# Busy matmuls and moved moments in the lead-in between two attentions

## The chip, the core and the metric

One NeuronCore of a Trainium2 chip runs the whole kernel. The metric is the device time of one execution in microseconds; the figure shown is the median of three runs. Five engines work side by side and meet at semaphores: TensorE (PE) multiplies, VectorE (DVE) and ScalarE (ACT) do elementwise work and reductions, GpSimd (POOL) helps, and SyncE (SP) issues the DMAs. TensorE's clock has two levels, 1.2 and 2.4 GHz, and the profile records which one was granted.

## What is computed

The input x is 4 batches of 1024 tokens of width 128, 32 tiles of 128 tokens. Cut to what matters:

```
x = x + layernorm(attention_1(layernorm(x)))
x = x + layernorm(attention_2_and_experts(layernorm(x)))

attention_1(s): q, k, v = tanh(s Wq + bq), tanh(s Wk + bk), tanh(s Wv + bv)   # 16 heads of 64
                a = softmax(causal(q k' / sqrt(64)));  return tanh(a v Wo + bo)
attention_2(h): Q, K, V = h q_w + q_b, h k_w + k_b, h v_w + v_b               # 16 heads, 4 wide
                m = softmax(Q K' / sqrt(4)) V o_w + o_b
                return h + 0.3 * (top 2 of 8 experts applied to m)
```

The layernorms have no weights: mean and variance over 128 columns, then (x - mean) / sqrt(var + 1e-5).

## The kernel before

The first attention goes through 32 pairs of heads (8 pairs in each of 4 batches, `N1` = 32). While pair i is worked on, the parts of pairs i-1 and i-2 are finished. `output(n)` on TensorE (L617 to L632, 24 matmuls at L631) multiplies the context of pair n by its rows of Wo into the PSUM banks `PJ`; `add_output(n)` on VectorE (L911 to L922) adds `PJ` to `acc` and counts `acc_added`. From pair 10 on one tile of `acc` per pair is finished (tanh, moments, normalise, add to X), so 22 of 32 tiles (`NORMED`) are done when the pairs end and ten (`LEFT`) are left.

The second attention goes through 16 groups of four heads, each with 32 items. In an item TensorE computes a block of maxima for the group ahead (two matmuls, L1943), two half blocks of scores (L1918) and one block of values (L1932); VectorE takes the maximum of each block (`read_item`, L2419); ScalarE takes two exponentials (L2177). TensorE computes the maxima of item u only when the reduce of item u-2 is done. The first group's maxima run 22 items (`LEAD`) ahead of its scores, so the first 22 blocks must be done before group 0 starts. They are done in the lead-in between the attentions by another path, `maxima_ahead`, `differences_ahead` and `quads_ahead`: for each pair of blocks k (blocks 2k and 2k+1), TensorE runs eight matmuls (L1291), ScalarE takes an absolute value of the first block (L1306, a difference), and VectorE combines it with the second in two instructions (L1317, a quad). There are three PSUM places for the blocks. Block m waits for the quad of block m-3 if m is even, and for the difference of block m-3 if m is odd.

Every engine works strictly in the order of the program text, which is written out by hand. At the end of the first attention the lead-in's steps are put between the last outputs. TensorE has in addition `keep_busy(count)` (L1295 to L1298): matmuls of the identity by itself into the first 128 columns of `PJ`, whose result nobody reads. Each is float32 and appears as two instructions in the trace. Since they write `PJ`, they have to wait until VectorE has read it.

In the kernel before:
- TensorE (end of `first_tensor`, then `second_tensor`, L2133 to L2138): blocks 0 to 3, 10 busy matmuls, blocks 4 and 5, 10 busy matmuls, output 30, blocks 6 to 9, output 31, blocks 10 to 13, a wait for the last addition, then four times 2 busy matmuls and two blocks, then `turn_tops(0, 0)` (L1952, transposes for the first scores) and the groups.
- ScalarE (L2253 to L2260): differences 4 to 7, a wait for the last addition, tanh of the ten left tiles at once (L2256), differences 8 to 10.
- VectorE (end of `first_vector`, then L2542 to L2545): quads 0 to 3 between the last additions, quads 4 to 9, `lower_queries` (L2428, the query correction, which needs `turn_tops`), quad 10, the groups.
- In group 0 `later_moments` (L2506 to L2520) gives VectorE, beside the reduces, ten `bn_stats` of the left tiles at items 2 to 11 (L2498), their `bn_aggr` at items 4 to 13 (L2515), and six `bn_stats` of tiles 16 to 21 of X at items 14 to 19. ScalarE normalises the ten left tiles at items 18 to 27 (L2213).

Of the kernel before, what the change touches and what calls it, by code (L numbers as in the profile page):

```python
# [24 lines left out]
T = S // P  # L25
# [4 lines left out]
N1 = B * PAIRS  # L30
# [52 lines left out]
def build(nc, states, Wq, bq, Wk, bk, Wv, bv, Wo, bo, q_w, q_b, k_w, k_b, v_w, v_b, o_w, o_b,  # L83
# [7 lines left out]
    with ExitStack() as ctx:  # L91
        def sb(name, shape, dt=F32):
            return ctx.enter_context(nc.sbuf_tensor(name, shape, dt))

        def sem(name):
            return ctx.enter_context(nc.semaphore(name))
# [15 lines left out]
        X = sb("X", [P, NT, D])  # L112
        acc = sb("acc", [P, NT, D])
# [3 lines left out]
        stats = sb("stats", [P, NT, 6])  # L117
# [277 lines left out]
        ctx_ready, wo_done, acc_added = sem("ctx_ready"), sem("wo_done"), sem("acc_added")  # L395
# [9 lines left out]
        NORMED = N1 - NORM_FROM  # L405
# [17 lines left out]
        def at_least(i, n):  # L423

            return not isinstance(i, int) or i >= n
# [6 lines left out]
        pow2, stats2, rstd2, hs_ready, d2 = sem("pow2"), sem("stats2"), sem("rstd2"), sem("hs_ready"), sem("d2")  # L432
# [80 lines left out]
        def first_tensor(pe):  # L513
# [205 lines left out]
            maxima_ahead(pe, 4, 6)  # L719
            keep_busy(pe, 10)  # L720
            output(N1 - 2, 0)
            maxima_ahead(pe, 6, 10)
            output(N1 - 1, 1)

        def first_scalar(act):
# [180 lines left out]
        def first_vector(dve):  # L906
# [4 lines left out]
            def add_output(n):  # L911

                dve.wait_ge(wo_done, n + 1)
                if at_least(n, 1):
                    dve.wait_ge(acc_added, n)
                if not at_least(n, 2):
                    dve.wait_ge(acc_begun, (1, B)[n])
                if isinstance(n, int):
                    v = acc[:, (n // PAIRS) * T:(n // PAIRS + 1) * T, :]
                else:  # L920
                    v = acc[:, bass.ds((n // PAIRS) * T, T), :]
                nc.vector.tensor_tensor(v, PJ.rearrange("p (t c) -> p t c", t=T), v, ALU.add).then_inc(acc_added, 1)  # L922
# [32 lines left out]
            def low_ctx(n, par):  # L955
                dve.wait_ge(ctx_hi_done, n + 1)
                nc.vector.tensor_tensor(ctx_lo[par], ctxT[par], ctx_hi[par], ALU.subtract).then_inc(ctx_ready, 1)
# [143 lines left out]
            ahead = Steps(dve, d2)  # L1101
# [9 lines left out]
            quads_ahead(dve, 2, 3)  # L1111
            low_ctx(N1 - 1, 1)
            quads_ahead(dve, 3, 4)
            add_output(N1 - 1)


# [33 lines left out]
        LEFT = NT - NORMED  # L1150
# [3 lines left out]
        left_tanh, left_stats, left_pow, left_normed, left_added = (  # L1154
            sem("left_tanh"), sem("left_stats"), sem("left_pow"), sem("left_normed"), sem("left_added"))
# [23 lines left out]
        ITEMS = 32  # L1179
        LEAD = 22  # L1180
        LEFT_AT, LEFT_NORM_AT = 2, 18
        MOMENTS_AT, LATER_MOMENTS_AT, ALL_MOMENTS_AT = 14, 8, 16
        LAST_MOMENTS_AT = 22

        TAIL = ITEMS - LEAD
# [66 lines left out]
        def tops_by(n, m):  # L1252

            if is_first(n) and m < LEAD:
                return m // 2 + 1
            return ITEMS * n + m + 1 - LEAD // 2
# [16 lines left out]
        def maxima_ahead(pe, first, end):  # L1273

            for m in range(first, end):
                qt, pr, kh = m // 4, m // 2 % 2, m % 2
                if m == 0:
                    pe.wait_ge(qk_in[0], 16 * 2 * GH)
                    pe.wait_ge(minus_ready, 1)
                    pe.wait_ge(exp_done, 5 * N1)  # L1280
                elif m == 2:
                    pe.wait_ge(out_copied, N1)
                elif m >= 3 and m % 2 == 1:
                    pe.wait_ge(gap_ready, (m - 3) // 2 + 1)
                elif m >= 3:
                    pe.wait_ge(top_done, tops_by(0, m - 3))
                dst = AHEAD[m % 3]
                for e, k in enumerate((k_rows[0][:, 0:HALF], k_rows[0][:, HALF:] if kh else k_minus)):
                    for i in range(2):
                        rows = slice(ROWS * (2 * pr + i), ROWS * (2 * pr + i + 1))  # L1290
                        last = nc.tensor.matmul(dst[:, i * HALF:(i + 1) * HALF], q_rows[0][rows, qt * P:(qt + 1) * P],  # L1291
                                                k[rows, :], start=(e == 0), stop=(e == 1))
                last.then_inc(mx_done, 1)

        def keep_busy(pe, count, dst=PJ):  # L1295

            for _ in range(count):
                nc.tensor.matmul(dst[:, 0:P], ident[:, :], ident[:, :], start=True, stop=True, skip_group_check=True)  # L1298

        def differences_ahead(act, first, end):  # L1300

            for k in range(first, end):
                act.wait_ge(mx_done, 2 * k + 1)
                if k >= 2:
                    act.wait_ge(top_done, k - 1)
                nc.scalar.activation(gap[k % 2].rearrange("p i c -> p (i c)"), AHEAD[2 * k % 3], ACT.Abs).then_inc(gap_ready, 1)  # L1306

        def quads_ahead(dve, first, end):

            for k in range(first, end):  # L1310
                qt, pr = k // 2, k % 2
                dve.wait_ge(gap_ready, k + 1)
                dve.wait_ge(mx_done, 2 * k + 2)
                v, src = gap[k % 2], AHEAD[(2 * k + 1) % 3]
                for i, done in ((0, gap_half), (1, top_done)):
                    at = 2 * pr + i
                    nc.vector.tensor_tensor_reduce(  # L1317
                        out=v[:, i, :], in0=src[:, i * HALF:(i + 1) * HALF], in1=v[:, i, :], scale=0.5,
                        scalar=LOWEST, op0=ALU.add, op1=ALU.max, accum_out=half_tops[:, 0, qt, at:at + 1]
                        ).then_inc(done, 1)  # L1320
                if k == T - 1:
                    find_tops(dve, 0, 0, k + 1)
# [569 lines left out]
        def second_tensor(pe):  # L1892
# [237 lines left out]
                    elif at_least(n, 1):  # L2130
                        values(n - 1, 1 - par, ITEMS + u - 2)

            maxima_ahead(pe, 10, 14)  # L2133
            pe.wait_ge(acc_added, N1)
            for m in range(14, LEAD, 2):
                keep_busy(pe, 2)
                maxima_ahead(pe, m, m + 2)
            turn_tops(0, 0)  # L2138
            each_group(pe, group)
# [19 lines left out]
        def second_scalar(act):  # L2159
# [90 lines left out]
                    if last and u == ITEMS - 1:  # L2250
                        exponentials(act, 0)

            differences_ahead(act, 4, 8)  # L2253
            act.wait_ge(acc_added, N1)
            left = acc[:, NORMED:, :]
            nc.scalar.activation(left, left, ACT.Tanh, scale=1.0 / WSCALE).then_inc(left_tanh, 1)  # L2256
            differences_ahead(act, 8, LEAD // 2)
            act.wait_ge(sum_lo, SUM_LO * N1)
            act.wait_ge(sum_hi, SUM_HI * N1)
            each_group(act, group)  # L2260
# [149 lines left out]
        def second_vector(dve):  # L2410
            steps, tops_steps = Steps(dve, d2), Steps(dve, d4)
# [85 lines left out]
            def statistics(src, t):  # L2497
                steps.done(nc.vector.bn_stats(stats[:, t, :], src[:, t, :]))  # L2498
# [5 lines left out]
            def later_moments(n, u):  # L2504

                if n == 0:  # L2506
                    j = u - LEFT_AT
                    if 0 <= j < LEFT:
                        if j == 0:
                            dve.wait_ge(left_tanh, 1)  # L2510
                        statistics(acc, NORMED + j)
                    j -= 2
                    if 0 <= j < LEFT:
                        dve.wait_ge(d2, 2 * T + j + 1)
                        last = nc.vector.bn_aggr(left_mv[:, j, :], stats[:, NORMED + j, :])  # L2515
                        if j == LEFT - 1:
                            last.then_inc(left_stats, 1)
                    j = u - MOMENTS_AT
                    if 0 <= j < NORMED - 2 * T:
                        statistics(X, 2 * T + j)  # L2520
                elif n == 1:
                    j = u - LATER_MOMENTS_AT
                    if 0 <= j < 3 * T - NORMED:
                        if j == 0:
                            dve.wait_ge(left_added, 1)
                        statistics(X, NORMED + j)
                    j = u - ALL_MOMENTS_AT
                    if 0 <= j < T:
                        last = input_moments_of(2 * T + j)
                        if j == T - 1:  # L2530
                            last.then_inc(stats2, 1)
                else:
                    j = u - LAST_MOMENTS_AT
                    if 0 <= j < T:
                        if n == 2:
                            statistics(X, 3 * T + j)
                        else:
                            last = input_moments_of(3 * T + j)
                            if j == T - 1:
                                last.then_inc(stats2, 1)  # L2540

            quads_ahead(dve, 4, LEAD // 2 - 1)  # L2542
            lower_queries(0, 0)
            quads_ahead(dve, LEAD // 2 - 1, LEAD // 2)
            steps.n = 2 * T  # L2545
            each_group(dve, group)
            third_vector(dve, normalise, add_projected, tops_steps)

# [49 lines left out]
```

## Time and profile before

| | us |
|---|---|
| median of three runs | 1599.55 |
| lowest, highest | 1599.39, 1603.34 |
| the profiled execution | 1599.43 |
| its span | 1597.60 |
| TensorE busy | 1522.4 (95%) |
| VectorE busy | 1419.8 (89%) |
| ScalarE busy | 1234.2 (77%) |
| GpSimd busy | 397.1 (25%) |

The span is what the trace covers; the profiled execution's own time is that and what lies around it. Busy shares are averages over stages with different limits. The first attention ends at about 742 us (the last addition), and group 0 of the second begins with the reduce at 757.32 us. In the timeline a row is one instruction or a run of like ones: start, length, engine, line, operation, output and input with their sizes, how many, and in brackets the idle time of the engine before it and what ended it.

### The profile page before, as it was taken

Reading aid. Unit: us, or ns where it says so; the run is one execution under the profiler, and the core shown is the slowest. Engines: PE = TensorE matmul, PEld = TensorE weight load, DVE = VectorE, ACT = ScalarE, POOL = GpSimd, SP = SyncE. Lnnn points to the kernel's source line nnn. Section 1 sums busy time; section 2 is a strip of 40 time slices with the busy share of each in tenths; the row PEclk is TensorE's granted clock in tenths of the full one; section 3 lists DMA queues with packets and bytes.
Section 4 is the critical chain, followed back from the end, with each engine's and each line's share of the span. In section 5 each row is a group of like instructions: output and inputs, shape, how many; then the busy total and the mean of one; then the engine's idle time right before and its main releaser. Section 6 shows DMA issues by size and latency. Waiting matters only on the chain.

```text
span 1597.6 us, 38714 instructions
## 1 busy us (share of the span) xinstructions
PE 1522.4 (95%) x14772; PEld 686.2 (43%) x14772; DVE 1419.8 (89%) x2198; ACT 1234.2 (77%) x1698; POOL 397.1 (25%) x563
## 2 busy tenths in 40 slices
PE   7899999999999999998899999999999999989996
PEld 3344444444444444444233333333333333466774
DVE  6888888888888888998999999999999999497888
ACT  4677777677777666774898999899989999766776
POOL 3311111221112222223235242324332432120004
PEclk9999999999999999997999999999999999999998
DMA  5311101111110111002012000200030000000001
GB/s 149 75 39 41 38 23 41 40 39 39 38 39 22 39 39 40 22 15 53 1 42 54 14 17 21 54 16 18 15 81 15 15 30 1 1 8 8 14 14 53
DMA packets 46606, 52.98 MB, mean 33 GB/s; under 512 B 9279, under 2 KB 33551, under 8 KB 46482
## 3 DMA queue, kind: packets, MB, share of 16 engines
q1 hardware_dynamic: 45584, 50.05, 10.7%
q8 instruction: 84, 1.38, 0.3%
q10 hardware_dynamic: 898, 1.22, 0.3%
q14 instruction: 40, 0.33, 0.1%
HBM read 15.07 MB, written 10.49 MB: 16 GB/s over the span
## 4 chain that ended last, share of the span: by engine, by line
PE 65%; DVE 20%; ACT 9%; issue 3%; POOL 1%; ACTq 0%; POOLq 0%; DVEq 0%
DVE arena L2419 16%; PE psum L592 16%; PE psum L573 12%; ACT arena L2177 7%; PE psum L1932 6%; PE psum L535 5%; PE psum L1563 5%; PE psum L1530 4%; PE psum L631 3%; PE psum L1943 3%; PE psum L609 2%; PE psum L1918 1%; PE psum L555 1%; PE psum L556 1%; PE psum L557 1%
## 5 line engine op out<-in xcount | busy, mean ns | idle before, releaser
L2419 DVE TENSOR_REDUCE arena<-psum 128x2 f32<-128x1024 f32 x490 | 566.1, 1218 | 10.4 <-PE psum L1943 8.8
L2177 ACT ACTIVATE arena<-psum 128x512 f32<-128x512 f32 x980 | 519.6, 600 | 51.2 <-PE psum L1918 45.3
L754 ACT ACTIVATE arena<-psum 128x2048 f32<-128x2048 f32 (+1 forms) x160 | 273.2, 1708 | 156.5 <-PE psum L573 156.5
L1932 PE MATMUL psum<-arena 128*32 128x256 f32 x4096 | 328.7, 393 | 1.5 <-ACT arena L2197 0.2
L592 PE MATMUL psum<-arena,hs 128*64 128x512 f32 (+3 forms) x1536 | 276.4, 495 | 0.0
L1918 PE MATMUL psum<-arena 32*128 32x512 bf16 x1024 | 256.8, 387 | 0.8 <-DVE arena L2419 0.2
L858 POOL TENSOR_SCALAR_AFFINE_SELECT arena<-arena 128x512 f32<-128x512 f32 (+1 forms) x160 | 99.9, 643 | 533.0 <-ACT arena L754 532.9
L573 PE MATMUL psum<-arena 64*128 64x512 f16 (+3 forms) x2304 | 216.2, 325 | 2.1 <-DVE arena L909 1.6
L1943 PE MATMUL psum<-arena 32*128 32x512 bf16 x980 | 191.5, 387 | 19.6 <-DVE arena L2419 11.2
L592 PEld LDWEIGHTS psum<-arena,hs 128*64 128x64 f32 x1536 | 96.7, 136 | 157.7 <-issue 149.7
L573 PEld LDWEIGHTS psum<-arena 64*128 64x128 f16 x2304 | 96.9, 94 | 134.2 <-issue 34.0
L1943 PEld LDWEIGHTS psum<-arena 32*128 32x128 bf16 x980 | 46.2, 91 | 233.0 <-DVE arena L2419 186.9
L909 DVE TENSOR_TENSOR arena<-arena 128x1024 f16<-128x1024 f32 x64 | 78.3, 1224 | 66.5 <-ACT arena L733 66.4
L1932 PEld LDWEIGHTS psum<-arena 128*32 128x32 f32 x4096 | 81.7, 108 | 113.6 <-issue 94.4
L1636 ACT ACTIVATE arena<-psum,b1T 128x1024 f16<-128x1024 f32 x64 | 71.3, 1115 | 51.0 <-PE psum L1530 48.4
L992 DVE TENSOR_TENSOR arena<-arena 128x1024 f32<-128x1024 f32 (+2 forms) x96 | 93.0, 969 | 9.2 <-POOL arena L858 5.0
L2339 POOL TENSOR_TENSOR arena<-arena,minus_one 128x16 f32<-128x16 f32 x30 | 87.1, 2905 | 54.7 <-ACT arena L2203 54.4
L1563 PE MATMUL psum<-arena 128*128 128x128 f16 x1536 | 92.6, 221 | 7.2 <-issue 5.4
L1563 PEld LDWEIGHTS psum<-arena 128*128 128x128 f16 x1536 | 89.5, 99 | 16.0 <-issue 8.7
L1918 PEld LDWEIGHTS psum<-arena 32*128 32x128 bf16 x1024 | 79.1, 91 | 37.6 <-ACT arena L2177 15.8
L535 PE MATMUL psum<-arena 128*128 128x512 f16 x384 | 93.8, 381 | 0.7 <-ACT hs L739 0.4
L1409 DVE TENSOR_TENSOR arena<-arena 128x1024 f16<-128x1024 f32 x59 | 71.7, 1222 | 22.4 <-ACT arena L1637 22.2
(223 smaller groups left out, 2013.5 us busy)
## 6 DMA issues: line engine op xcount, KB each, us to landing
arena<-arena SPq DMA_DIRECT2D x30, 512.0 KB, 2.9
arena<-arena SPq DMA_DIRECT2D x46, 128.0 KB, 2.2
arena<-latent_q SPq DMA_DIRECT2D x64, 64.0 KB, 2.0
arena<-latent_k SPq DMA_DIRECT2D x64, 64.0 KB, 2.0
arena<-arena SPq DMA_DIRECT2D x60, 64.0 KB, 2.4
X<-in_L_attn_states SPq DMA_DIRECT2D x4, 512.0 KB, 4.4
latent_q<-arena SPq DMA_DIRECT2D x16, 96.0 KB, 2.3
latent_k<-arena SPq DMA_DIRECT2D x16, 96.0 KB, 2.4
```

Source lines behind the costliest of these rows:

```text
L535: last = nc.tensor.matmul(dst[:, half * HALF:(half + 1) * HALF], w_now[:, 2 * j + w, :], x_now[:, x, half * HALF:(half + 1) * HALF], start ...
L573: last = nc.tensor.matmul(SC[:, s, c:c + w], k[rows, kt * P:(kt + 1) * P], q[rows, q0:q0 + w], start=(m == 0), stop=(m == 2), skip_group_c ...
L592: last = nc.tensor.matmul(OUT[s * DH:(s + 1) * DH, q0:q0 + w], vals[par][:, kt, s * DH:(s + 1) * DH], probs[g][:, s, c:c + w], start=first ...
L754: nc.scalar.activation(probs[g], SC[:, :, 0:WIDTH[g]], ACT.Exp, scale=DH ** -0.5).then_inc(exp_done, 1)
L858: return nc.gpsimd.affine_select(out=v, in_=v, compare_op=ALU.is_ge, fill=0.0, base=0, pattern=[[0, blocks], [1, P]], channel_multiplier=-1)
L992: nc.vector.tensor_tensor(v, v, probs[3][:, :, c:c + n], ALU.add).then_inc(sum_hi, 1)
L1563: last = nc.tensor.matmul(YP[slot][:, tok], h[slot][c][:, tok], w2_e[par][:, w, c, :], start=(c == 0 and m == 0), stop=(c == FC - 1 and m ...
L1918: return nc.tensor.matmul(dst, k_rows[par][rows, kt * P:(kt + 1) * P], q_rows[par][rows, h * HALF:(h + 1) * HALF], start=True, stop=True)
L1932: last = nc.tensor.matmul(OT[ROWS * c:ROWS * (c + 1), h * HALF // 2:(h + 1) * HALF // 2], v_cols[par][:, kt, 2 * pr + i, :], e_probs[u % 4 ...
L1943: last = nc.tensor.matmul(dst[:, i * HALF:(i + 1) * HALF], q_rows[par][rows, qt * P:(qt + 1) * P], k_rows[par][rows, kh * HALF:(kh + 1) * ...
L2177: nc.scalar.activation(e_probs[u % 4][:, i * HALF:(i + 1) * HALF], ring(n, u, i), ACT.Exp, scale=KD ** -0.5).then_inc(e_done, 1)
L2419: nc.vector.tensor_reduce(half_tops[:, kh, qt, 2 * pr:2 * pr + 2], src.rearrange("p (i c) -> p i c", i=2), AX.X, ALU.max).then_inc(top_don ...
```

## The change

- TensorE: blocks 6 and 7, a wait for the addition of output 30, 16 busy matmuls, blocks 8 and 9, output 31. After it blocks 10 and 11, the wait for the last addition, then five times 12 busy matmuls and two blocks (it was four times 2).
- VectorE: the six `bn_stats` of X tiles 16 to 21 stand before the last addition. The ten of the left tiles stand between quads 6 and 10 in portions of 2, 2, 3 and 3, behind a wait for ScalarE's tanh. In group 0 only the ten `bn_aggr` stay, at items 2 to 11, two items earlier.
- ScalarE: the tanh of the left tiles comes after difference 5 and no longer after difference 7.
- `lower_queries` stays between quads 9 and 10.

```diff
--- before.py
+++ after.py
@@ -719,7 +719,10 @@
             maxima_ahead(pe, 4, 6)
             keep_busy(pe, 10)
             output(N1 - 2, 0)
-            maxima_ahead(pe, 6, 10)
+            maxima_ahead(pe, 6, 8)
+            pe.wait_ge(acc_added, N1 - 1)
+            keep_busy(pe, 16)
+            maxima_ahead(pe, 8, 10)
             output(N1 - 1, 1)
 
         def first_scalar(act):
@@ -1111,6 +1114,8 @@
             quads_ahead(dve, 2, 3)
             low_ctx(N1 - 1, 1)
             quads_ahead(dve, 3, 4)
+            for t in range(2 * T, NORMED):
+                ahead.done(nc.vector.bn_stats(stats[:, t, :], X[:, t, :]))
             add_output(N1 - 1)
 
 
@@ -1179,7 +1184,7 @@
         ITEMS = 32
         LEAD = 22
         LEFT_AT, LEFT_NORM_AT = 2, 18
-        MOMENTS_AT, LATER_MOMENTS_AT, ALL_MOMENTS_AT = 14, 8, 16
+        LATER_MOMENTS_AT, ALL_MOMENTS_AT = 8, 16
         LAST_MOMENTS_AT = 22
 
         TAIL = ITEMS - LEAD
@@ -2130,10 +2135,10 @@
                     elif at_least(n, 1):
                         values(n - 1, 1 - par, ITEMS + u - 2)
 
-            maxima_ahead(pe, 10, 14)
+            maxima_ahead(pe, 10, 12)
             pe.wait_ge(acc_added, N1)
-            for m in range(14, LEAD, 2):
-                keep_busy(pe, 2)
+            for m in range(12, LEAD, 2):
+                keep_busy(pe, 12)
                 maxima_ahead(pe, m, m + 2)
             turn_tops(0, 0)
             each_group(pe, group)
@@ -2250,11 +2255,11 @@
                     if last and u == ITEMS - 1:
                         exponentials(act, 0)
 
-            differences_ahead(act, 4, 8)
+            differences_ahead(act, 4, 6)
             act.wait_ge(acc_added, N1)
             left = acc[:, NORMED:, :]
             nc.scalar.activation(left, left, ACT.Tanh, scale=1.0 / WSCALE).then_inc(left_tanh, 1)
-            differences_ahead(act, 8, LEAD // 2)
+            differences_ahead(act, 6, LEAD // 2)
             act.wait_ge(sum_lo, SUM_LO * N1)
             act.wait_ge(sum_hi, SUM_HI * N1)
             each_group(act, group)
@@ -2506,18 +2511,10 @@
                 if n == 0:
                     j = u - LEFT_AT
                     if 0 <= j < LEFT:
-                        if j == 0:
-                            dve.wait_ge(left_tanh, 1)
-                        statistics(acc, NORMED + j)
-                    j -= 2
-                    if 0 <= j < LEFT:
-                        dve.wait_ge(d2, 2 * T + j + 1)
+                        dve.wait_ge(d2, 2 * T + NORMED - 2 * T + j + 1)
                         last = nc.vector.bn_aggr(left_mv[:, j, :], stats[:, NORMED + j, :])
                         if j == LEFT - 1:
                             last.then_inc(left_stats, 1)
-                    j = u - MOMENTS_AT
-                    if 0 <= j < NORMED - 2 * T:
-                        statistics(X, 2 * T + j)
                 elif n == 1:
                     j = u - LATER_MOMENTS_AT
                     if 0 <= j < 3 * T - NORMED:
@@ -2539,10 +2536,22 @@
                             if j == T - 1:
                                 last.then_inc(stats2, 1)
 
-            quads_ahead(dve, 4, LEAD // 2 - 1)
+            def left_moments(first, end):
+                for t in range(first, end):
+                    statistics(acc, NORMED + t)
+
+            steps.n = NORMED
+            quads_ahead(dve, 4, 7)
+            dve.wait_ge(left_tanh, 1)
+            left_moments(0, 2)
+            quads_ahead(dve, 7, 8)
+            left_moments(2, 4)
+            quads_ahead(dve, 8, 9)
+            left_moments(4, 7)
+            quads_ahead(dve, 9, 10)
+            left_moments(7, LEFT)
             lower_queries(0, 0)
-            quads_ahead(dve, LEAD // 2 - 1, LEAD // 2)
-            steps.n = 2 * T
+            quads_ahead(dve, 10, LEAD // 2)
             each_group(dve, group)
             third_vector(dve, normalise, add_projected, tops_steps)
```

## Rows read from the trace of the kernel before

**Rows 1.** The page's slices: granted TensorE clock in tenths, 40 equal slices.

```profile
PEclk9999999999999999997999999999999999999998
```

**Rows 2.** Windows: stretch, length, busy PE, PEld, DVE, ACT, POOL, granted clock, DMA.

```profile
734.90:738.30 3.40, 1.28 (x13) 0.58 (x14) 3.40 (x7) 2.21 (x3) 0.00 (x0) 1.00 0.00 0
738.30:741.70 3.40, 3.40 (x29) 2.44 (x28) 1.91 (x5) 0.31 (x2) 0.00 (x0) 0.50 0.00 0
741.70:745.10 3.40, 2.40 (x20) 1.03 (x18) 2.86 (x10) 1.95 (x2) 0.00 (x0) 1.00 0.29 93
745.10:748.50 3.40, 3.40 (x18) 1.52 (x14) 2.52 (x9) 2.25 (x3) 0.25 (x1) 0.50 0.56 135
...
762.20:765.60 3.40, 3.40 (x32) 0.73 (x28) 3.22 (x6) 2.40 (x5) 0.00 (x0) 0.50 0.00 0
```

**Rows 3.** The chain of waits around 750 us: start, length, engine, line, instructions.

```profile
747.42 1.82 PE psum L1291 x8
...
749.24 1.15 PE psum L1298 x4
```

**Rows 4.** Timeline, TensorE's and VectorE's steps from 728 to 756 us: start, length, work.

```profile
728.95 1.04 PE L1291 MATMUL psum<-arena 32*128 32x512 bf16 x8
...
729.91 2.50 PE L1298 MATMUL psum<-ident 128*128 128x128 f32 x20
...
732.25 1.50 PE L631 MATMUL psum<-arena 128*128 128x128 f16 x24
...
733.68 1.03 PE L1291 MATMUL psum<-arena 32*128 32x512 bf16 x8
...
734.34 1.22 DVE L922 TENSOR_TENSOR acc<-psum,acc 128x1024 f32<-128x1024 f32 x1
...
738.06 2.53 PE L631 MATMUL psum<-arena 128*128 128x128 f16 x24 [0.19 <-DVE arena L957]
...
740.62 1.22 DVE L922 TENSOR_TENSOR acc<-psum,acc 128x1024 f32<-128x1024 f32 x1 [1.49 <-PE psum L631]
...
755.12 0.61 PE L1952 MATMUL psum<-identb,arena 128*128 128x128 bf16 x4
```

**Rows 5.** Timeline, ScalarE's difference, and VectorE's hand-over to group 0.

```profile
729.59 1.02 ACT L1306 ACTIVATE arena<-psum 128x1024 f32<-128x1024 f32 x1 [1.42 <-PE psum L1291]
...
755.77 0.42 DVE L2428 TENSOR_TENSOR arena<-psum,arena 128x512 bf16<-128x512 bf16 x1 [2.00 <-PE psum L1952]
...
756.11 0.68 DVE L1317 CUSTOM_DVE_ANT_0 arena<-psum,arena 128x512 f32<-128x512 f32 x1
...
757.32 3.48 DVE L2419 TENSOR_REDUCE arena<-psum 128x2 f32<-128x1024 f32 x3
```

**Rows 6.** Timeline of VectorE in group 0: reduces of the maxima, one an item.

```profile
761.38 1.22 DVE L2419 TENSOR_REDUCE arena<-psum 128x2 f32<-128x1024 f32 x1 [0.38 <-PE psum L1943]
...
762.94 1.23 DVE L2419 TENSOR_REDUCE arena<-psum 128x2 f32<-128x1024 f32 x1
...
767.34 1.19 DVE L2419 TENSOR_REDUCE arena<-psum 128x2 f32<-128x1024 f32 x1
...
768.73 1.19 DVE L2419 TENSOR_REDUCE arena<-psum 128x2 f32<-128x1024 f32 x1
...
774.50 1.20 DVE L2419 TENSOR_REDUCE arena<-psum 128x2 f32<-128x1024 f32 x1
...
775.70 1.20 DVE L2419 TENSOR_REDUCE arena<-psum 128x2 f32<-128x1024 f32 x1
```

**Rows 7.** Windows, all engines, of group 0 and later; then line 2419 alone.

```profile
757.32:785.15 27.83, 24.01 (x238) 6.52 (x238) 27.24 (x51) 22.52 (x45) 3.73 (x8) 0.85 0.01 1
...
785.15:798.19 13.04, 12.37 (x128) 3.54 (x122) 12.36 (x13) 12.63 (x29) 4.96 (x7) 1.00 0.01 1
...
918.00:958.00 40.00, 38.38 (x424) 13.28 (x423) 39.19 (x39) 36.41 (x73) 16.74 (x24) 1.00 0.05 15
...
785.15:798.19 13.04, 11.86 (x10) 1.00 0.01 1
```

## The prediction

> **What bounds the kernel now.** I read the page's line of the granted clock first [rows 1]. It is full in every slice but the nineteenth (7) and the last (8, the kernel's end), so the change can earn something in one place only, some 25 us around 750 us. Next I cut that place into equal stretches [rows 2]. TensorE had work for 1.28 of 3.40 us in 734.90:738.30, and the next stretch ran at 0.50, the 1.2 GHz level. The one after, behind 3.40 us of work that is mostly the dense matmuls of the output (L631), ran at 1.00 (2.4 GHz). In that stretch it was busy for 2.40 us, mostly with the thin 32-row maxima, and from 745.10 on the clock is 0.50 until 765.60, so the low time is 3.4 + 20.5 = 23.9 us.
>
> Then the chain of waits [rows 3]. From 744 to 755 us it stays on TensorE and alternates between eight maxima matmuls (1.82 us) and four instructions of keep_busy(2) (1.15 us): one pair of maxima costs 2.97 us at the low clock. The timeline gives the same work at the full clock [rows 4]: maxima 4 and 5 take 728.95 to 729.91, 0.96 us; keep_busy(10), which is 20 instructions because each f32 matmul is two, takes 729.91 to 732.25, 0.117 us an instruction; the output takes 732.25 to 733.68, 1.43 us. Last, VectorE in group 0 of the second attention [rows 6, 7]: from the first reduce at 757.32 to 785.15 us it is busy 27.24 of 27.83 us, so it and not TensorE is the bound there even while the clock is low. From then to 798.19 ScalarE is (12.63 of 13.04 us, in which ten reduces pass, 1.30 us each).
>
> **The lead-in, step by step.** Nothing before maxima 8 changes. I follow TensorE's order from there, at the full clock, and weigh the clock afterwards.
> - Maxima 6 and 7 begin at 733.68 and end 0.96 us later. The new wait for the addition of output 30 ends when that VectorE instruction does, 734.34 + 1.22 = 735.56 [rows 4]. keep_busy(16), 32 instructions, takes 3.74 us: 735.6 to 739.36. In the kernel before, TensorE stood idle for part of this time, waiting for a quad, then ran maxima 8 and 9 and began output 31 at 738.06. Behind the wait stand just these two, and for them wait ScalarE's difference 4 and VectorE's last addition.
> - Maxima 8 and 9 to 740.32, output 31 to 741.8. Its addition starts 0.03 us behind the last matmul in the rows (738.06 + 2.53, 740.62) and takes 1.22 us: 743.05. Maxima 10 and 11 fit beside it. The six moments put ahead of this addition cost nothing: the row at 740.62 shows VectorE idle for 1.49 us before it, since 739.13, so 1.2 us of moments end by 740.4, ahead of 741.8. If the output were early again, as at 740.62, they would still just fit.
> - From 743.15, five rounds of keep_busy(12) and two maxima. A round is 24 x 0.117 + 0.96 = 3.77 us, five are 18.85 us, so turn_tops starts at 762.0. It started at 755.12: **6.9 us later**. The old rounds were four, cheaper even at the low clock (2.97 us), because they held 4 busy instructions and not 24.
> - Within a round VectorE has a quad of 1.21 us (756.11 to 757.32, [rows 5]) and two or three moments of 0.19 us, at most 1.8 us, and ScalarE one difference of 1.02 us; both fit in 3.77 us, so the ten moments are free here. If the busy matmuls weren't there they would still fit in 2.97 us. ScalarE's tanh moved ahead of difference 6 runs from 743.6 to 744.9, while TensorE is busy until 746; VectorE's wait for it (in front of the first moments, with quad 7 behind) ends before maxima 15, so it costs nothing either. Without that cover it would be its own 1.26 us; I take 0, bounds 0 to 1.3.
> - Hand-over to group 0. Before: turn_tops at 755.12, the query correction at 755.77, quad 10 at 756.11, first reduce at 757.32: 2.20 us [rows 4, 5]. At the full clock turn_tops is over about 0.25 us sooner; quad 10 needs difference 10: block 20 begins at 761.04, a difference starts 0.64 us behind its blocks (728.95, 729.59) and takes 1.02, so it ends at 762.7. So the correction runs 762.4 to 762.78, quad 10 to 764.0, and the first reduce is at 764.0: **6.7 us later** than before.
> - GpSimd's split of the first tops and the normal inputs behind it move with maxima 15, by some 4.5 us, and are over before group 0 asks GpSimd for anything. SP's loads of the next group's rows wait for the last addition and move by 1.2 us; they are used ten items into the group. Both 0; a late load would show as a wait at item 10 and cost at most 1 us.
>
> **Group 0.** An item with a moment and an aggregate takes 768.73 - 767.34 = 1.39 us, one with an aggregate alone 775.70 - 774.50 = 1.20 us [rows 6], so a moment is worth 0.19 us. A bare reduce takes about 1.14 us (three at 757.32 take 3.48 us, overlaps in it, [rows 5]). Sixteen leave. The last two stand at items 18 and 19, where ScalarE starts to set the pace of 1.30 us with the ten left tiles, so only fourteen count: 14 x 0.19 = 2.7 us. The 0.6 us in which VectorE stood idle come on top where the clock is full. A faster VectorE gets less tightly fed: later groups show it idle for 0.81 of 40 us [rows 7], 0.4 us over 22 us. I take 0.3. Group 0 gives back **3.0 us**, between 2.3 (no idle regained, 0.4 lost) and 3.7 (all sixteen moments and the idle).
>
> **The clock.** In the new order the stretch that let it fall (1.28 of 3.40 us) holds about 2.7 us of dense work, and each round of 3.77 us holds 2.81 us of it, so I take the full clock for the lead-in. Its start of group 0 is another matter: turn_tops, maxima 22 and the first scores are thin, and TensorE waits for the correction and quad 10, about 1.5 us of 3.4. The stretch of [rows 2] that was busy for 2.40 us with mostly thin work was followed by a fall, so one at 765 us is more likely than not. At the low clock an item took 1.56 us of TensorE (the reduces at 761.38 and 762.94, [rows 6]) against 1.22 us for VectorE, so each 3.4 us costs 2.2 x 0.34 = 0.75 us. Bounds 0 and 1.5 (two such stretches); I take 0.4.
>
> **Sum.** 6.7 - 3.0 + 0.4 = 4.1 us later. The profiled execution's own time is 1599.43 us, 1.83 us around a span of 1597.60, and the median of the runs shown is 1599.55, the same within 0.01%. So 1603.5 us. Its own range, with the terms' bounds, is 1602 to 1606. A measurement of this kernel tells about 0.3% (4.8 us) from no change; 4.1 us lies just inside it.
>
> **Rivals.**
> - *The clock falls all the same* (ends slower). Busy matmuls come too late or too few, and TensorE drops to 1.2 GHz before or within the rounds. Mechanism and place: each 3.4 us of low clock among the rounds does half the work, 1.7 us lost, because a round is all TensorE. It decides as soon as one such stretch is there, since 4.1 + 1.7 = 5.8 us passes 4.8. Two of them give 1607 us. For it: the clock fell twice here with TensorE 38% and 70% busy. Against: 3.40 us of output matmuls brought it back at once. If the rounds ran low from end to end, 24 instructions and eight maxima at the old rates are 24 x 0.2875 + 1.82 = 8.7 us and the kernel would be near 1628 us.
> - *The low stretch is paid back by half.* If TensorE set the pace throughout the 23.9 us, the full clock gives back 12.0 us. The busy matmuls go from 8 to 16 + 60 = 76; the 68 more, 136 instructions x 0.117, cost 15.9, of which 1.2 fill old idle time, and the moments give 3.0: 15.9 - 1.2 - 12.0 - 3.0 = -0.3, so 1599.2 us. Against it: VectorE was the bound from 757 us on, and the rounds' wait for dense work.
> - *Busy matmuls hide* (ends faster). If the rounds went at VectorE's and ScalarE's pace and not TensorE's, 1.9 us a round (a quad, three moments, latency), the lead-in would be 5 x 1.87 = 9.3 us shorter than summed: 1594.2 us. It needs TensorE to take 24 instructions in under 1 us, which no row shows; the 20 at 729.91 took 2.34 us and the output waited behind them.
>
> For the second rival the Trainium skill has a rule (TensorE: Matmul & The Clock Gate, Terms): the price of a throttled time is about that time multiplied by one minus the granted share. By it alone the change would come out level. The trace disagrees for the part after 757 us, where VectorE was idle for 0.59 us only.
>
> **How the numbers follow.** The forecast gets 0.55: 0.37 of it within 4.8 us and 0.18 above. The clock that falls anyway 0.20, all slower. Half paid back 0.15, all no change. Hidden busy matmuls 0.10, all faster. That makes faster 0.10, no change 0.52, slower 0.38. The range 1598.5 to 1609 leaves out the hidden case and the worst of the falling clock.
>
> **What would show it.** keep_busy(16) from 735.6 us for 3.7 us; five pairs of maxima 3.8 us apart with a granted clock of 1.00; turn_tops near 762; the first reduce near 764; a wait of TensorE for the last addition of some 0.3 us; items of group 0 at 1.20 us; moments between the quads with idle time around them. The prediction is wrong if the clock line still shows a low slice, if rounds are much shorter than 3.7 us, or if group 0 still takes 25 us from its first reduce to item 18.

## The result, and the profile after

The changed kernel takes 1607.52 us (median of 19 runs, 1603.16 to 1609.94) where the kernel before, measured beside it, takes 1602.14 (19 runs, 1598.65 to 1609.28). The ratio is 1.0027, 95% interval [1.0017, 1.0037]: 4.3 us slower (2.7 to 5.9), and 4.1 were forecast; the two medians by themselves differ by 5.4. Its profiled execution has a span of 1601.6 us, 4.0 more than before. The changed kernel's times scatter by 7 us and those of the kernel before by 11; the places in which their traces differ are shown below.

The page's line of the granted clock, 40 slices, answers to [rows 1]. The 7 in the nineteenth slice is gone:

```profile
PEclk9999999999999999999999999999999999999998
```

Windows of the changed kernel (stretch, length, busy PE, PEld, DVE, ACT, POOL, granted clock, DMA), answering to [rows 2] and [rows 7]:

```profile
734.90:738.30 3.40, 3.40 (x32) 3.40 (x31) 3.40 (x10) 0.46 (x1) 0.00 (x0) 1.00 0.01 2
742.25:761.47 19.22, 19.22 (x160) 15.31 (x161) 9.79 (x35) 5.86 (x7) 7.56 (x14) 1.00 0.29 69
761.47:763.47 2.00, 1.11 (x10) 0.41 (x8) 1.56 (x6) 1.28 (x3) 0.00 (x0) 1.00 0.00 0
...
766.50:769.75 3.25, 3.25 (x32) 0.62 (x24) 3.25 (x7) 2.40 (x5) 0.00 (x0) 0.50 0.00 0
763.47:795.05 31.58, 29.17 (x301) 8.38 (x301) 31.05 (x41) 29.17 (x61) 3.74 (x8) 0.95 0.01 1
```

The stretch in which the clock fell before holds 3.40 us of work, and the clock is full through all five rounds (742.25 to 761.47). TensorE is busy in each microsecond of them, VectorE for 9.79 of 19.22. In the hand-over to group 0 it has little to do (1.11 of 2.00 us), and a low stretch follows at 766.5, too short for the page's line of slices.

TensorE's timeline (start, length, work), answering to [rows 4]:

```profile
732.76 1.04 PE L1296 MATMUL psum<-arena 32*128 32x512 bf16 x8
734.68 3.84 PE L1303 MATMUL psum<-ident 128*128 128x128 f32 x32 [0.89 <-DVE acc L925]
738.46 1.03 PE L1296 MATMUL psum<-arena 32*128 32x512 bf16 x8
739.42 1.51 PE L631 MATMUL psum<-arena 128*128 128x128 f16 x24
740.87 1.03 PE L1296 MATMUL psum<-arena 32*128 32x512 bf16 x8
742.25 2.94 PE L1303 MATMUL psum<-ident 128*128 128x128 f32 x24 [0.35 <-DVE acc L925]
745.13 1.04 PE L1296 MATMUL psum<-arena 32*128 32x512 bf16 x8
746.10 2.94 PE L1303 MATMUL psum<-ident 128*128 128x128 f32 x24
...
760.50 1.04 PE L1296 MATMUL psum<-arena 32*128 32x512 bf16 x8
761.47 0.40 PE L1957 MATMUL psum<-identb,arena 128*128 128x128 bf16 x4
```

A round is the step from one start to the next: 746.10 - 742.25 = 3.85 us, and from 742.25 to turn_tops at 761.47 it is 19.22 us. VectorE's timeline, answering to [rows 5, 6]:

```profile
738.12 1.25 DVE L1118 BATCH_NORM_STATS2 stats<-X 128x6 f32<-128x128 f32 x6
740.97 1.23 DVE L925 TENSOR_TENSOR acc<-psum,acc 128x1024 f32<-128x1024 f32 x1 [1.60 <-PE psum L631]
...
748.06 0.48 DVE L2503 BATCH_NORM_STATS2 stats<-acc 128x6 f32<-128x128 f32 x2
750.68 0.69 DVE L1322 CUSTOM_DVE_ANT_0 arena<-psum,arena 128x512 f32<-128x512 f32 x1 [2.13 <-ACT arena L1311]
...
763.47 3.48 DVE L2424 TENSOR_REDUCE arena<-psum 128x2 f32<-128x1024 f32 x3
...
766.95 1.20 DVE L2424 TENSOR_REDUCE arena<-psum 128x2 f32<-128x1024 f32 x1
...
768.15 1.19 DVE L2424 TENSOR_REDUCE arena<-psum 128x2 f32<-128x1024 f32 x1
...
780.51 14.50 DVE L2424 TENSOR_REDUCE arena<-psum 128x2 f32<-128x1024 f32 x12
795.05 0.17 DVE L1333 TENSOR_TENSOR arena<-arena 128x16 f32<-128x16 f32 x1
```

The six moments of X end 1.60 us ahead of output 31's end, so they cost nothing; two moments stand behind quad 6 with idle time after them. In group 0 the reduces come every 1.20 us, and the line at 795.05 is the combination of maxima after item 25. In the trace before it stands here:

```profile
792.18 0.17 DVE L1328 TENSOR_TENSOR arena<-arena 128x16 f32<-128x16 f32 x1
```

### The profile page after: what moved, and what is told of

The parts are those of the page before. It is cut to its first block, busy times and chain, and to the rows that moved or that the text cites. A ratio compares the mean times of both kernels' runs of the same rounds, so it can differ in the third digit from the quotient of the medians.

```text
span 1601.6 us, 38986 instructions
## 1 busy us (share of the span) xinstructions
PE 1529.6 (96%) x14908; PEld 698.9 (44%) x14908; DVE 1419.8 (89%) x2198; ACT 1233.7 (77%) x1698; POOL 397.2 (25%) x563
## 3 DMA queue, kind: packets, MB, share of 16 engines
q10 hardware_dynamic: 898, 1.22, 0.3%
## 4 chain that ended last, share of the span: by engine, by line
PE 65%; DVE 21%; ACT 9%; issue 2%; POOL 1%; ACTq 0%; POOLq 0%; DVEq 0%
DVE arena L2424 17%; PE psum L592 16%; PE psum L573 12%; ACT arena L2182 7%; PE psum L1937 5%; PE psum L535 5%; PE psum L1568 5%; PE psum L1535 4%; PE psum L631 3%; PE psum L1948 3%; PE psum L609 2%; PE psum L1303 1%; PE psum L1923 1%; PE psum L555 1%; PE psum L557 1%
```

## Where the 4 us are

The two traces differ by 0.9 us in the first attention already, so I count from block 6, the last step ahead of anything changed. All times are differences of starts in the timeline, and the last column runs from the last reduce to the end of the span:

| | block 6 to turn_tops | block 6 to first reduce | first reduce to item 25's | block 6 to item 25's | last reduce to end |
|---|---|---|---|---|---|
| before | 21.44 | 23.64 | 34.86 | 58.50 | 244.1 |
| changed | 28.71 | 30.71 | 31.58 | 62.29 | 245.2 |
| changed, second trace (E7) | 28.71 | 30.70 | 32.63 | 63.33 | 247.8 |
| changed, third trace (E8) | 28.72 | 30.72 | 32.63 | 63.35 | 247.9 |
| E1 busy matmuls alone | 28.72 | 30.71 | 33.94 | 64.65 | 245.5 |
| E2 moments alone | 21.37 | 23.58 | 33.18 | 56.76 | 247.8 |
| E3 rounds of 5 | 20.91 | 22.90 | 31.75 | 54.65 | 244.1 |
| E4 rounds of 2 | 23.86 | 26.06 | 32.55 | 58.61 | 244.0 |
| E5 rounds of 5, no 16 | 19.21 | 21.20 | 31.89 | 53.09 | 244.0 |
| E6 rounds of 4 | 19.91 | 21.95 | 31.58 | 53.53 | 248.2 |
| E9 rounds of 5, no 16, six later | 21.34 | 23.34 | 31.73 | 55.07 | 244.0 |
| E10 the same with rounds of 3 | 25.97 | 28.18 | 32.79 | 60.97 | 244.1 |

From item 25's combination to the last reduce every one of these traces takes 561.3 to 561.5 us. So the change is the fourth column, 62.29 - 58.50 = 3.8 us, made of 7.1 us of lead-in less 3.3 us of group 0. The two parts of the change, taken singly below, give 6.15 us (E1) and -1.74 us (E2), 4.4 together. The last column is the third stage, which no kernel here touches, and it differs by up to 4.2 us. It goes with the granted clock of 1360 to 1440 us: 0.98 in the six traces with 244.0 or 244.1 us, 0.96 in the two with 245.2 and 245.5, and 0.91 in the four with 247.8 to 248.2.

## The experiments

**E1, the busy matmuls alone.**

```diff
-            maxima_ahead(pe, 6, 10)
+            maxima_ahead(pe, 6, 8)
+            pe.wait_ge(acc_added, N1 - 1)
+            keep_busy(pe, 16)
+            maxima_ahead(pe, 8, 10)
...
-            for m in range(14, LEAD, 2):
-                keep_busy(pe, 2)
+            for m in range(12, LEAD, 2):
+                keep_busy(pe, 12)
```

> Only TensorE's part of the change: the wait, 16 busy matmuls, and five rounds of 12, with VectorE's and ScalarE's text as before. My theory: the rounds are TensorE's alone, so the first reduce of group 0 comes some 6.7 to 7.1 us later than before (counted from block 6), and group 0 gets nothing back but VectorE's 0.6 us of idle time: 6.5 us later than before, ratio 1.004. The rival that the low stretch is paid back by half expects 2.7 us (15.9 - 1.2 - 12.0); the rival that busy matmuls hide expects a gain of some 6 us.

Measured: 1605.66 us against 1601.56, ratio 1.0031 [1.0017, 1.0045]. VectorE's timeline:

```profile
763.70 3.48 DVE L2422 TENSOR_REDUCE arena<-psum 128x2 f32<-128x1024 f32 x3
...
797.64 0.17 DVE L1331 TENSOR_TENSOR arena<-arena 128x16 f32<-128x16 f32 x1
```

Block 6 is at 732.99 in this trace. The first reduce is 7.07 us later than before, and group 0 is 0.9 us shorter: block 6 to item 25 is 6.15 us longer. Both rivals are refuted by the trace, since they expected 2.7 us and a gain; the ratio's interval (2.7 to 7.2 us) alone would leave the first at its edge.

**E2, the moments alone.** VectorE's and ScalarE's part of the change on TensorE's old text.

```diff
-            maxima_ahead(pe, 6, 8)
-            pe.wait_ge(acc_added, N1 - 1)
-            keep_busy(pe, 16)
-            maxima_ahead(pe, 8, 10)
+            maxima_ahead(pe, 6, 10)
...
-            maxima_ahead(pe, 10, 12)
+            maxima_ahead(pe, 10, 14)
...
-            for m in range(12, LEAD, 2):
-                keep_busy(pe, 12)
+            for m in range(14, LEAD, 2):
+                keep_busy(pe, 2)
```

> Only the moved moments and ScalarE's earlier tanh, with TensorE's text as before (2 busy matmuls in four rounds, low clock). My theory: group 0 is 3 us shorter, the lead-in is not longer because VectorE has room in each round, so 3 us faster than before, ratio 0.998. The clock stays low to about 765 us, and group 0's first items then fall from VectorE's pace of 1.39 us to TensorE's of 1.56 us, which may take back up to 1.5 us. A rival in which the moments' place is worth nothing expects no difference.

Measured: 1599.41 us, ratio 0.9989 [0.9976, 1.0001]. The lead-in is not longer, as TensorE's timeline shows (the same 2.97 us from the maxima of one round to those of the next, 1.81 + 1.16 us, as in [rows 3]):

```profile
746.99 1.89 PE L1293 MATMUL psum<-arena 32*128 32x512 bf16 x8
748.80 1.22 PE L1300 MATMUL psum<-ident 128*128 128x128 f32 x4
749.96 1.89 PE L1293 MATMUL psum<-arena 32*128 32x512 bf16 x8
```

Group 0 gives 1.7 us back, not 3. Its first items at the low clock come every 1.56 us, TensorE's pace. So the moments are worth 1.7 us beside a low clock and 33.94 - 31.58 = 2.4 us beside a mostly full one (E1 against the changed kernel's first trace; against its other two, in which the clock is low for longer, 1.3). The interval of E2's times includes no difference.

**E3, rounds of 5.** The changed kernel with fewer busy matmuls in a round.

```diff
             for m in range(12, LEAD, 2):
-                keep_busy(pe, 12)
+                keep_busy(pe, 5)
```

> The changed kernel with 5 busy matmuls in a round and not 12. My theory, TensorE bound at the full clock: a round is 10 x 0.117 + 0.96 = 2.13 us and not 3.77, five are 8.2 us shorter, so 4 us faster than before and 8 us faster than the changed kernel, ratio to before 0.9975. If the clock needs more dense work than that to stay, rounds of 10 x 0.2875 + 1.82 = 4.7 us come up and the time is that of the changed kernel or worse.

Measured: 1595.69 us (1594.75 to 1596.71 in 9 runs), ratio 0.996 [0.9947, 0.9973]. TensorE's timeline:

```profile
744.25 1.38 PE L1303 MATMUL psum<-ident 128*128 128x128 f32 x10 [0.35 <-DVE acc L925]
745.57 1.03 PE L1296 MATMUL psum<-arena 32*128 32x512 bf16 x8
746.53 1.38 PE L1303 MATMUL psum<-ident 128*128 128x128 f32 x10
...
754.69 1.03 PE L1296 MATMUL psum<-arena 32*128 32x512 bf16 x8
755.66 0.40 PE L1957 MATMUL psum<-identb,arena 128*128 128x128 bf16 x4
```

The round is 2.28 us (744.25 to 746.53) and the clock stays full to turn_tops. Block 6 to turn_tops is 7.8 us shorter than in the changed kernel: seven matmuls a round, 14 instructions of 0.117 us, five times, is 8.2. This shows that the rounds' dense filling is what the change pays for, and that twelve are not needed to hold the clock. To item 25 this trace is 58.50 - 54.65 = 3.9 us shorter than the kernel before; the times say 6.4 (4.3 to 8.5), and E3 was profiled in the longest of its nine executions, the kernel before in one of its shorter ones.

**E4, rounds of 2.** As E3 with `keep_busy(pe, 2)`.

> The changed kernel with 2 busy matmuls in a round. If the full clock holds, TensorE needs 0.47 + 0.96 = 1.43 us and VectorE 1.21 us for a quad and 0.4 to 0.6 us for its moments, so VectorE sets about 1.8 us a round: 9.8 us shorter than the changed kernel, 5.7 us faster than before, ratio 0.9964. I think it more likely that the clock falls, as it did at 745 us before with the same rounds; then rounds take 2.97 us, turn_tops comes 4 us sooner than in the changed kernel, and the total is that of the kernel before.

Measured: 1594.14 us, ratio 0.996 [0.9944, 0.9975], in two groups: seven runs from 1592.66 to 1594.30 with mean granted clocks of 0.992 to 0.995, and five from 1598.21 to 1599.61 with 0.988 to 0.990. The profiled run is of the second group. Its TensorE timeline:

```profile
739.70 1.51 PE L631 MATMUL psum<-arena 128*128 128x128 f16 x24
741.15 1.03 PE L1296 MATMUL psum<-arena 32*128 32x512 bf16 x8
742.53 0.71 PE L1303 MATMUL psum<-ident 128*128 128x128 f32 x4 [0.35 <-DVE acc L925]
743.75 1.31 PE L1296 MATMUL psum<-arena 32*128 32x512 bf16 x8 [0.51 <-DVE arena L1322]
744.99 1.22 PE L1303 MATMUL psum<-ident 128*128 128x128 f32 x4
746.15 1.89 PE L1296 MATMUL psum<-arena 32*128 32x512 bf16 x8
...
756.89 0.61 PE L1957 MATMUL psum<-identb,arena 128*128 128x128 bf16 x4
```

The first round begins at the full clock; from the second on eight maxima take 1.89 us and four busy instructions 1.22. No trace shows the faster group, so that the clock held in its lead-in is inferred: in the profiled execution block 6 comes within 0.5 us of the earliest of all traces and the third stage is the shortest seen (244.0 us), item 25 to the last reduce is alike everywhere, and only the lead-in and the start of group 0 are left for 5 us. On this reading both of my alternatives came true, in different executions of one program.

**E5, rounds of 5 without the 16.**

```diff
             pe.wait_ge(acc_added, N1 - 1)
-            keep_busy(pe, 16)
             maxima_ahead(pe, 8, 10)
...
-                keep_busy(pe, 12)
+                keep_busy(pe, 5)
```

> Rounds of 5 busy matmuls, but without the 16 busy matmuls ahead of block 8 (the wait for the addition of output 30 stays). My theory: blocks 8 and 9 wait for quad 2 as they did before, so output 31 begins 1.3 us sooner after block 6 than with the 16; the clock falls at about 738 us as it did before, output 31 runs at the low level (2.5 us and not 1.5) and brings it back, so turn_tops comes at most 0.5 us sooner than in the kernel with both (19.9 us after it in place of 20.9), and the time is 1595 to 1596 us, within 0.1% of it. The rival: the 16 are what keeps the clock for the rounds; without them the rounds of 5 run low for some time, 2 to 8 us more, and the runs scatter.

Measured: 1594.55 us (1593.38 to 1596.43, only 5 runs), ratio 0.9956 [0.9939, 0.9973]. The clock did not fall at 738 us in this trace, so output 31 took 1.50 us and turn_tops came 19.21 us after block 6, 1.7 sooner than in E3. I had expected the fall. E9, in which TensorE's text is the same, shows it: the 16 busy matmuls take away a chance of a fall and not a sure one.

**E6, rounds of 4.** As E3 with `keep_busy(pe, 4)`.

> Four busy matmuls in a round. A round at the full clock is 0.96 + 8 x 0.117 = 1.90 us against 2.28 us measured for five (TensorE), and VectorE's 1.6 to 1.8 us fits: five rounds are 1.2 to 1.9 us shorter, 1594.2 us. The rival, that less dense work in a round lets the clock fall in some executions as with two, expects two groups of times, 1594 and 1599 us.

Measured: 1596.21 us (1593.59 to 1598.01, 6 runs), ratio 0.996 [0.9943, 0.9977]. The lead-in is 1.0 us shorter than with five (1.2 to 1.9 were expected), with a full clock in the trace. The median is 2.0 us above the expected 1594.2 and not lower than E3's. The profiled execution, the slowest of the six, has the long third stage (248.2 us); whether others had it, or lost the clock in the rounds, stays open.

**E7 and E8, the changed kernel again, for two more traces.**

> The changed kernel once more, for another trace: its times lie in two groups, near 1603.5 and 1607.7 us, with mean granted clocks of 0.994 and 0.989. If this one is of the later group, its trace shows where the clock is low: my theory is one of the places outside the lead-in (20 to 60 or 1360 to 1430 us), since each round holds 2.8 us of dense work; the rival is the lead-in itself, rounds longer than 3.84 us.

> The same once more, for the same question: a time near 1603.5 us with the clock full throughout the lead-in, or near 1607.7 us with a low stretch whose place the trace shows. My theory puts it outside the lead-in, the rival inside it.

Measured: 1606.95 and 1607.08 us, both near the slower of the two times. (The nineteen runs of the changed kernel do not fall into two clear groups; some lie between, as 1604.73 and 1605.67.) VectorE's timeline of E7:

```profile
763.32 3.48 DVE L2424 TENSOR_REDUCE arena<-psum 128x2 f32<-128x1024 f32 x3
...
766.95 1.22 DVE L2424 TENSOR_REDUCE arena<-psum 128x2 f32<-128x1024 f32 x1
...
768.51 1.23 DVE L2424 TENSOR_REDUCE arena<-psum 128x2 f32<-128x1024 f32 x1 [0.25 <-PE psum L1948]
...
770.07 1.23 DVE L2424 TENSOR_REDUCE arena<-psum 128x2 f32<-128x1024 f32 x1 [0.24 <-PE psum L1948]
...
795.95 0.17 DVE L1333 TENSOR_TENSOR arena<-arena 128x16 f32<-128x16 f32 x1
```

Line 2424 alone (instructions, shortest, median, longest; first and last start), in the changed kernel's first trace and in E7:

```profile
L2424 DVE TENSOR_REDUCE arena<-psum x490: 1190/1218/1226, 763.5 to 1356.4; 128x2 f32<-128x1024 f32 x164
```

```profile
L2424 DVE TENSOR_REDUCE arena<-psum x490: 1191/1219/1226, 763.3 to 1357.3; 128x2 f32<-128x1024 f32 x164
```

The lead-in is the same to 0.02 us, so the rival that puts the difference there is refuted. Of 3.5 us of span, 1.05 come in group 0, where the items from 766.95 to 770.07 go at TensorE's low pace of 1.56 us (the granted clock from the first reduce to item 25 is 0.90, and 0.95 in the first trace), and 2.6 between the last reduce and the end: 1605.1 - 1357.3 = 247.8 against 1601.6 - 1356.4 = 245.2.

**E9, the six moments behind the last addition.** E5 with

```diff
-            for t in range(2 * T, NORMED):
-                ahead.done(nc.vector.bn_stats(stats[:, t, :], X[:, t, :]))
             add_output(N1 - 1)
+            for t in range(2 * T, NORMED):
+                ahead.done(nc.vector.bn_stats(stats[:, t, :], X[:, t, :]))
```

> Rounds of 5 busy matmuls, without the 16, and the six moments of X behind the last addition and not ahead of it. Without the 16, VectorE's six moments ended at 739.6 us while output 31 was over at 738.9, so they held the last addition and with it the first round. My theory: moved behind it they lie in VectorE's wait for difference 6, the first round begins 0.6 to 0.7 us sooner, and the kernel is 0.6 us faster than that one: 1594.0 us. The rival, that the third stage's scatter of up to 4 us covers it, expects no difference in the times, but the trace still shows turn_tops 18.6 us behind block 6 and not 19.2.

Measured: 1596.11 us (1594.70 to 1597.31, 9 runs), ratio 0.9962 [0.995, 0.9975]. The expectation missed; turn_tops came 21.34 us after block 6 and not 18.6. TensorE's timeline:

```profile
737.04 1.04 PE L1295 MATMUL psum<-arena 32*128 32x512 bf16 x8 [2.21 <-DVE arena L1321]
738.17 2.20 PE L631 MATMUL psum<-arena 128*128 128x128 f16 x24
...
742.12 2.50 PE L1302 MATMUL psum<-ident 128*128 128x128 f32 x10
...
746.02 1.38 PE L1302 MATMUL psum<-ident 128*128 128x128 f32 x10
...
755.14 0.40 PE L1956 MATMUL psum<-identb,arena 128*128 128x128 bf16 x4
```

The clock fell while output 31 ran (2.20 us and not 1.50), and the first round took 3.90 us, the later ones 2.28. Moving the six moments could not be judged against that.

**E10, the same with rounds of 3.**

> The same with 3 busy matmuls in a round. At the full clock a round would be 1.66 us for TensorE and up to 1.8 us for VectorE, so five rounds take 9 us and not 11.4: turn_tops 16.5 us behind block 6, 2 us faster, 1592 us. With 0.7 us of dense work in 1.8 us I expect the clock to fall in part of the executions, which then take 4 us more, as with two busy matmuls; if none falls, the highest time stays under 1596 us.

Measured: 1605.28 us (1600.78 to 1607.36, 12 runs), ratio 1.0017 [1.0003, 1.003]: a miss, and in every run. TensorE's timeline:

```profile
737.43 2.72 PE L631 MATMUL psum<-arena 128*128 128x128 f16 x24
...
741.46 0.94 PE L1302 MATMUL psum<-ident 128*128 128x128 f32 x6
...
748.82 1.65 PE L1302 MATMUL psum<-ident 128*128 128x128 f32 x6
750.40 1.89 PE L1295 MATMUL psum<-arena 32*128 32x512 bf16 x8
...
759.02 0.61 PE L1956 MATMUL psum<-identb,arena 128*128 128x128 bf16 x4
```

Every round but the first is at the low clock: six busy instructions 1.58 us and eight maxima 1.82, 3.40 us together. No run of twelve has a mean granted clock above 0.986. E4 has fewer busy matmuls in a round but the 16 ahead of them, and seven of its twelve runs are at 0.992 or more. E10 differs from it in the place of the six moments too. The cleaner comparison is E2, which differs from E4 only on TensorE, by the 16 with their wait and by one round of 2 more: none of its twelve runs is above 0.987. So the 16 do seem to matter where the rounds are weak (no run takes them out by themselves with rounds of two); with rounds of five (E3, E5, E9) the clock holds or comes back within a round.

## Why the prediction was right, step by step

- *Where the clock is low.* The forecast read the line of slices as full everywhere but around 750 us and at the end. A 9 there is 90% or more of 40 us, and finer windows of the kernel before show 0.91 over 40 to 60 us and over 1400 to 1420 us. Nothing in the sum rests on it, but the scatter of the times does.
- *keep_busy(16) and the wait.* Forecast 3.74 us from the end of an addition; it ran from 734.68, 0.05 us behind that end (733.41 + 1.22), for 3.78 us. Right.
- *Five rounds of 3.77 us.* 3.84 to 3.85 us each, 19.22 in all against 18.85. A batch costs a little more than the row of before said, where 20 instructions came out at 0.117 us each: 24 now come out at 0.120, and the 10 of E3 at 0.132. turn_tops is 7.3 us later, not 6.9, and the first reduce 7.1, not 6.7.
- *The moments are hidden in the lead-in.* Right: E2's turn_tops is 0.07 us earlier than before with all sixteen in. My aside that the six would "just fit" with an early output was wrong by 0.6 us: in E5, whose output ended at 738.9, they ended at 739.6 and held the last addition.
- *Group 0 gives 3.0 us back.* 3.3 in the changed kernel's profile and 2.2 in E7 and E8. Reduces with an aggregate come every 1.20 us, as forecast.
- *A fall of the clock at the start of group 0.* Forecast as likely, near 765 us, at 0.75 us for each low stretch. It is in all three traces. In the first it cost nothing against VectorE's pace; in the other two it lasted longer and cost 1.05 us. The 0.4 us lies between the two and is right for neither.
- *The sum.* 7.1 - 3.3 = 3.8 us in the first trace, 7.1 - 2.2 = 4.8 in the others; the ratio of the runs says 4.3, the forecast said 4.1. That the last two agree to 0.2 us is luck: the lead-in was 0.4 us longer than forecast, and group 0 gave back more or less than forecast by the execution.
- *The clock falls all the same.* Not with 12 in a round: in three traces the lead-in is full throughout. It is what E4 and E10 show with fewer.
- *The low stretch is paid back by half.* Refuted by E1 for group 0, and not for the lead-in. Of the 23.9 us of low clock 15.6 (3.4, and 745.10 to 757.32) lie before the first reduce, where TensorE was the bound for the most part; half of that is 7.8 us, and E1 gives 15.9 - 1.2 - 7.1 = 7.6 us back there. The other 8.3 us lie in group 0, where half would be 4.1 us, and E1 is only 0.9 us shorter: VectorE's idle time fell from 0.66 to 0.09 us and its busy time from 34.20 to 33.85. (About 1.7 of the 4.1 could not come back anyway, since E1's group 0 has a low stretch of its own, 0.95 over 33.94 us.) By an estimate with the Trainium skill's rule (TensorE: Matmul & The Clock Gate, Terms: throttled time multiplied by one minus the granted share) E1 should have been 2.7 us slower than before; its trace is 6.2. The trace agrees with the rule in the lead-in and not in group 0.
- *Busy matmuls hide.* Refuted by E1 and E3: seven matmuls fewer in a round take 7.8 us off five rounds.
- *The absolute time.* 1603.5 was worked out from a median of three runs, 1599.55. The kernel before has since shown medians of 1601.5 to 1602.1 in 10 to 32 runs, so 2.6 of the 4.0 us by which 1607.5 lies above the forecast are in the time of before, and the other 1.4 in the difference (5.4 between the medians and not 4.1). The median is above the forecast's own range of 1602 to 1606. The scatter goes with low stretches in the third stage and at the start of group 0: the last reduce to the end is 244.0 to 245.5 us in eight traces and 247.8 to 248.2 in four. In E7 and E8 the clock is below full in two places between 1360 and 1440 us (0.83 and 0.84 over 20 us), in E2 too (0.83 and 0.85), in the trace of before in one (0.91). All twelve traces go together in this, but no experiment changed the third stage, so that the clock is the cause there is argued, not shown.

Against the kernel before, E3 is the version to keep: 0.996 [0.9947, 0.9973], some 6 us faster, with a spread of 2 us. E4's median is lower, but five of its twelve runs are 2.5 to 4 us above E3's. E5's ratio is the same within the intervals and rests on five runs.

## What to carry to other kernels

Filling an engine's waits costs nothing only up to the length of the wait. Once the filler is the engine's own bound, each instruction of it is on the path, so price it by the row (0.117 us, and somewhat more in a small batch) and find the smallest count that keeps the clock. What a full clock gives back is only what the clocked engine, and not its neighbour, was holding up (here nearly half of the low time in the lead-in, and 0.9 of 8.3 us in group 0); read that from the neighbour's idle time. Read the same kernel in several traces before a step of 2 or 3 us is believed, and compare counts from the last common instruction.

## What the runs showed of the hardware that I had not expected

TensorE can be busy without a pause and still stay at 1.2 GHz: before, from 745.10 to 755.30 us, with thin maxima and four dense instructions a round, and in E10 from 745.40 to 757.20 us (11.80 of 11.80 us busy at 0.50) with six. With ten a round it went back to 2.4 GHz within the first round (E9). Two executions of one program can go different ways: in the changed kernel the clock is 0.50 from 764.60 to 768.00 us in E7, and 0.99 from 763.47 to 766.50 in the first trace, with the low stretch behind it. E4's times fall into two groups with middles of 1593.8 and 1598.8 us, by the inference above because the lead-in kept the clock in some runs and lost it in others; these 4.9 us are more than the whole change is worth.
